# Layer-2 tile conversions placed between the links of the first pair's LoRA chain, tile by tile in a mixed pair, with the first split and the layer-3 loads moved ahead

## The reference

```python
def _L0_cond_ref(x, weight, bias, lora_a_weights, lora_b_weights, scaling_factors, adapter_id):
    base = jnp.einsum('bsi,oi->bso', x, weight) + bias
    low = jnp.einsum('bsi,bri->bsr', x, lora_a_weights[adapter_id])
    delta = jnp.einsum('bsr,bor->bso', low, lora_b_weights[adapter_id])
    return base + scaling_factors[adapter_id][:, None, None] * delta
...
x = x + _L0_cond_ref(x, ..., itok_B_1_7)     # 8 adapters of rank 16
x = x + _L1_cond_ref(x, itok_B_6_15, ...)    # the same form, 32 adapters of rank 16, own weight and bias
x = x + einsum('bsi,boi->bso', x, weight2[itok_B_3_7])   # one of 8 matrices of 1024 x 1024
x = x + einsum('bct,bcd->bdt', x, weights3[itok_B_0_15]) # 64 x 64 on the row axis
```

## Time and profile before

| | us |
|---|---|
| median of 3 runs | 655.12 |
| lowest, highest | 651.77, 655.34 |
| profiled execution, its own time | 655.87 |
| its span in the trace | 653.7 |
| PE busy, share of the span | 612.1, 94% |
| DVE busy | 297.5, 46% |
| ACT busy | 214.4, 33% |
| POOL busy | 50.3, 8% |

### The profile page before, as it was taken

The page is one execution under the profiler, slowest core; times in us unless marked ns, Lnnn a source line. Parts: engine busy times, 40 slices in busy tenths (PEclk is TensorE's granted clock), DMA queues, the critical chain, the costliest instruction groups (busy, mean ns, idle before and its releaser), DMA issues.

```text
span 653.7 us, 10849 instructions
## 1 busy us (share of the span) xinstructions
PE 612.1 (94%) x2834; PEld 505.4 (77%) x2835; DVE 297.5 (46%) x554; ACT 214.4 (33%) x306; POOL 50.3 (8%) x87
## 2 busy tenths in 40 slices
PE   5999999999938999999999998999998989999994
PEld 4888878888827888878888887888887756888882
DVE  4992211040464558254356724544863473534210
ACT  3642211040351346222335422323642352333021
POOL 4220001000010011000002100000200030000000
PEclk7999999999987999999999998999999798999997
DMA  7655723021057325733323473233348342221102
GB/s 267 228 181 59 87 82 131 31 84 65 1 181 160 120 63 192 203 100 107 97 85 109 162 227 100 77 102 101 125 134 214 107 160 81 66 87 29 34 2 66
DMA packets 70620, 73.61 MB, mean 113 GB/s; under 512 B 43586, under 2 KB 51778, under 8 KB 70596
## 3 DMA queue, kind: packets, MB, share of 16 engines
q1 hardware_dynamic: 70596, 73.32, 38.8%
HBM read 62.03 MB, written 11.27 MB: 112 GB/s over the span
## 4 chain that ended last, share of the span: by engine, by line
issue 46%; PE 37%; DMA 6%; DVE 3%; POOLq 3%; SPq 2%; POOL 1%; ACT 1%; DVEq 0%; ACTq 0%
PE y_ps L975 10%; PE y_ps L1023 6%; PE t_ps L975 5%; PE y_ps L1052 4%; PE y_ps L957 3%; DMA arena<-wt 3%; POOLq L215 2%; DMA arena<-d_tab 2%; PE t_ps L957 2%; DVE ring L820 2%; PE low_ps L957 2%; PE t_ps L1074 1%; PE low_ps L1014 1%; PE t_ps L966 1%; POOL arena L428 1%
## 5 line engine op out<-in xcount | busy, mean ns | idle before, releaser
L1052 PE MATMUL y_ps<-ring,ops 128*128 128x512 f32 (+1 forms) x792 | 188.3, 394 | 4.0 <-DVE ring L820 3.9
L1023 PE MATMUL y_ps<-wm,ops 128*128 128x512 f32 x768 | 183.7, 396 | 0.0
L1052 PEld LDWEIGHTS y_ps<-ring,ops 128*128 128x128 f32 (+1 forms) x792 | 145.5, 186 | 38.5 <-DVE ring L820 4.8
L1023 PEld LDWEIGHTS y_ps<-wm,ops 128*128 128x128 f32 x768 | 146.1, 192 | 30.5
L975 PE MATMUL y_ps<-ring,wm 128*128 128x512 f32 x240 | 55.3, 390 | 0.0
L820 DVE TENSOR_TENSOR ring<-arena,ring 128x1024 fp32r<-128x1024 f32 x40 | 48.1, 1250 | 14.0 <-ACT ring L526 12.5
L778 DVE SCALAR_TENSOR_TENSOR ops<-arena,b_is_lo,ops 128x1040 fp32r<-128x1040 f32 x16 | 20.8, 1299 | 73.9 <-ACT ops L520 73.9
L975 PEld LDWEIGHTS y_ps<-ring,wm 128*128 128x128 f32 x240 | 44.9, 188 | 9.3
L526 ACT CAST ring<-arena 128x1024 fp32r<-128x1024 f32 x40 | 40.5, 1049 | 24.8 <-POOL arena L428 23.7
L766 DVE TENSOR_TENSOR ops<-arena,ops 128x512 fp32r<-128x512 f32 x32 | 21.9, 691 | 55.3 <-ACT ops L504 55.3
L520 ACT ACTIVATE ops<-arena,b_sign 128x1040 fp32r<-128x1040 f32 x16 | 18.7, 1166 | 82.6 <-DMA arena<-d_tab 81.3
(11 more groups left out here) (143 smaller groups left out, 572.5 us busy)
## 6 DMA issues: line engine op xcount, KB each, us to landing
arena<-wt SPq DMA_DIRECT2D x48, 512.0 KB, 5.4
arena<-b_tab SPq DMA_DIRECT2D x32, 256.2 KB
arena<-xt SPq DMA_DIRECT2D x32, 256.0 KB, 2.9
arena<-b_tab SPq DMA_DIRECT2D x32, 256.0 KB
out<-arena SPq DMA_DIRECT2D x30, 256.0 KB, 3.7
arena<-w SPq DMA_DIRECT2D x8, 576.0 KB, 4.1
a_stage<-a_tab SPq DMA_DIRECT2D x64, 64.0 KB, 1.9
arena<-a_cols SPq DMA_DIRECT2D x8, 256.0 KB, 2.7
```

Source lines behind the costliest of these rows:

```text
L1023: op = nc.tensor.matmul(y_ps[:, cols], xs[:, k, part_x, :], wm[:, k, part_w, cols], start=k == 0 and part_x == part_w, stop=False)
L1052: op = nc.tensor.matmul(y[0:m, cols], xs2[:, k, part_x, 0:m], ring[:, k, part_w, cols], start=k == 0 and part_x == part_w, stop=k == KT - ...
```

## The change

1. Pair 0: instead of `convert(0, range(KT))` after everything of step 0, ACT and DVE convert two tiles at a time at four places: (0, 1), (2, 3) and (4, 5) in step 0 (DVE does (4, 5) in step 1, behind `low(1, 0)`), and (6, 7) in step 1 behind `a_hi(2)` and `a_lo(2)`.
2. Mixed pair: `quarters` is replaced by `tile_used` (one increment a tile), `half_used` and `l2_done`; ACT's `convert_mixed` waits for each tile alone. `half_used` is given by the first matmul of the second half, which stands behind the transposes.
3. Launch: A columns have semaphores `a1_in` of their own and their cast stands ahead of the fold; PE's high-by-high products wait only for `w0_hi`; `w0_lo` comes before the `b0_side` part; `start_the_order` follows the slots; 11 warm-ups in place of 9.
4. SP: `load_w3(j-1)` stands before `store(j-2)`.

```diff
-WARM_UPS = 9
+WARM_UPS = 11
...
-                sp.dma_start(slot(k)[:, FEATS + N0_COLS:], a1_cols[k]).then_inc(slot_in[k % STAGES], 16)
+                sp.dma_start(slot(k)[:, FEATS + N0_COLS:], a1_cols[k]).then_inc(a1_in[k % STAGES], 16)
...
-                    store(j - 2)
                     sp.wait_ge(w3_lo_ready, j - 1)
                     load_w3(j - 1)
+                    store(j - 2)
...
-            store(PAIRS - 2)
             sp.wait_ge(w3_lo_ready, PAIRS - 1)
             load_w3(PAIRS - 1)
+            store(PAIRS - 2)
...
             for k in range(KT):
+                act.wait_ge(a1_in[k % STAGES], 16 * (k // STAGES + 1))
+                nc.scalar.copy(a1[:, k, 0, :], slot(k)[:, FEATS + N0_COLS:]).then_inc(a1_hi, 1)
                 act.wait_ge(w0_folded, k + 1)
-                nc.scalar.copy(a1[:, k, 0, :], slot(k)[:, FEATS + N0_COLS:])
-                nc.scalar.copy(w0_blocks(k, 0), slot(k)[:, 0:FEATS].rearrange("p (i m) -> p i m", m=P))
-                nc.scalar.copy(b0_side[:, 0, k, :], slot(k)[:, FEATS:FEATS + N0_COLS]).then_inc(w0_hi, 1)
+                nc.scalar.copy(w0_blocks(k, 0), slot(k)[:, 0:FEATS].rearrange("p (i m) -> p i m", m=P)).then_inc(w0_hi, 1)
+                nc.scalar.copy(b0_side[:, 0, k, :], slot(k)[:, FEATS:FEATS + N0_COLS]).then_inc(b0_hi, 1)
...
+            def convert_mixed(rank, j):
+
+                for k in range(KT):
+                    act.wait_ge(tile_used, KT * j + (k + 1))
+                    convert(rank + 1, (k,))
+
             def xs2_hi(j, h):
                 act.wait_ge(t_done, j + 1)
                 if not (isinstance(j, int) and j == 0):
-                    act.wait_ge(quarters, 4 * j + (h - 1))
+                    act.wait_ge((half_used, l2_done)[h], j)
...
                     second_half_of_next(j - 2)
+                if before == 0:
+                    act.wait_ge(product_done, DONE_M + KT)
+                    convert(0, (0, 1))
                 if not last:
                     a_hi(j + 1)
...
                 if before == 1:
+                    convert(0, (6, 7))
                     xs2_hi(0, 0)
                     xs2_hi(0, 1)
                 if not last:
-                    for h in range(2):
-                        x_hi(j + 1, h)
+                    x_hi(j + 1, 0)
+                    if before == 0:
+                        convert(0, (2, 3))
+                    x_hi(j + 1, 1)
                     b_hi_parts(j + 1)
                 if before == 0:
-                    act.wait_ge(product_done, DONE_M + KT)
-                    convert(0, range(KT))
+                    convert(0, (4, 5))
                     return
...
                 with act.If(mixed != 0):
-                    act.wait_ge(quarters, 4 * j - 3)
-                    convert(rank + 1, FIRST_HALF)
-                    act.wait_ge(quarters, 4 * j - 2)
-                    convert(rank + 1, SECOND_HALF)
+                    convert_mixed(rank, j - 1)
...
                 low(j, 0)
+                if before == 0:
+                    convert(0, (0, 1))
+                if before == 1:
+                    convert(0, (4, 5))
...
             masks()
-            start_the_order()
             for k in range(KT):
                 split_slot(k)
+            start_the_order()
...
             def a1_products():
                 for k in range(KT):
+                    pe.wait_ge(w0_hi, k + 1)
+                    for i in range(KT):
+                        nc.tensor.matmul(PASS1[i], wm[:, i, 0, k * P:(k + 1) * P], a1[:, k, 0, :], start=k == 0, stop=False)
                     pe.wait_ge(w0_lo, k + 1)
                     for i in range(KT):
-                        for part_w, part_a in SPLIT:
+                        for part_w, part_a in SPLIT[1:]:
...
+                            if final and k == HK and part_x == part_w and cols is BANKS[0]:
+                                op.then_inc(half_used, 1)
...
+                    if final and k == KT - 1:
+                        op.then_inc(l2_done, 1)
+                    elif tiles:
+                        op.then_inc(tile_used, 1)
```

More of the change, by code:

```diff
@@ L183, in build @@
         ones_ready = sem("ones_ready")
+        a1_in = [sem(f"a1_in{n}") for n in range(STAGES)]
         w0_folded, w0_hi, w0_lo = sem("w0_folded"), sem("w0_hi"), sem("w0_lo")
+        a1_hi, b0_hi, b0_lo = sem("a1_hi"), sem("b0_hi"), sem("b0_lo")
         w1_folded, w1_hi, w1_lo = sem("w1_folded"), sem("w1_hi"), sem("w1_lo")
@@ L209, in build @@
         t_done, xs2_hi_ready, xs2_lo_ready = sem("t_done"), sem("xs2_hi_ready"), sem("xs2_lo_ready")
-        quarters = sem("quarters")
+        tile_used, half_used, l2_done = sem("tile_used"), sem("half_used"), sem("l2_done")
         x3_hi_ready, x3_lo_ready = sem("x3_hi_ready"), sem("x3_lo_ready")
@@ L861, in step @@
                 if not last:
-                    for h in range(2):
-                        x_lo(j + 1, h)
+                    x_lo(j + 1, 0)
+                    if before == 0:
+                        convert(0, (2, 3))
+                    x_lo(j + 1, 1)
                 take_x2(j)
@@ L1046, in transposes, with layer2_half @@
                 op.then_inc(t_done, 1)
-            def layer2_half(y, h, m=P, marks=()):
+            def layer2_half(y, h, m=P, tiles=False, final=False):
                 for k in (FIRST_HALF, SECOND_HALF)[h]:
@@ L1053, in layer2_half @@
                                                   start=k == 0 and part_x == part_w, stop=k == KT - 1 and part_x == 1)
-                    if k in marks:
-                        op.then_inc(quarters, 1)
+                            if final and k == HK and part_x == part_w and cols is BANKS[0]:
+                                op.then_inc(half_used, 1)
+                            if tiles and final and k == KT - 1 and part_x == 1 and cols is BANKS[0]:
+                                op.then_inc(tile_used, 1)
+                    if final and k == KT - 1:
+                        op.then_inc(l2_done, 1)
+                    elif tiles:
+                        op.then_inc(tile_used, 1)
             def layer2_by_banks(y, m=P):
@@ L1088, in first_part @@
                     pe.wait_ge(w_lo, rank * KT + HK)
-                    layer2_half(y, 0, marks=marks)
+                    layer2_half(y, 0, tiles=True)
                     between()
@@ L1092, in first_part, with last_part @@
                     pe.wait_ge(w_lo, rank * KT + KT)
-                def last_part(m=P):
+                def last_part(m=P, tiles=False):
                     if last:
@@ L1097, in last_part @@
                     else:
-                        layer2_half(y, 1, m, marks=(KT - 1,))
+                        layer2_half(y, 1, m, tiles=tiles, final=True)
                 with pe.If(mixed != 0):
-                    first_part((HK - 1,))
-                    layer2_half(y, 1, marks=(KT - 1,))
+                    first_part()
+                    layer2_half(y, 1, tiles=True)
                     pe.wait_ge(w_lo, rank * KT + (KT + HK))
-                    layer2_half(y, 0, ROWS, marks=(HK - 1,))
+                    layer2_half(y, 0, ROWS)
                     pe.wait_ge(w_lo, rank * KT + (KT + KT))
@@ L1107, in layer2 @@
                 with pe.Else():
-                    first_part((HK - 3, HK - 2, HK - 1))
-                    last_part()
+                    first_part()
+                    last_part(tiles=True)
             def step(j, before=1):
```

31 lines of the change are left out of this document (16 added, 15 removed).

## The result

| | before | changed |
|---|---|---|
| median of 4 runs, us | 655.23 | 636.33 |
| lowest, highest | 651.77, 659.79 | 633.63, 637.75 |
| profiled execution | 655.87 | 633.63 |
| its span | 653.7 | 631.4 |

Each kernel has a fourth run here; with it the median before is 655.23. The changed kernel takes 0.9703 of the time before (95% interval 0.9633 to 0.9772): 19 us less by the medians, 22.2 by the two profiled executions, of which the changed one is the fastest of its four. The forecast was 629, with a range up to 636; the median lies 7 us above the forecast and 0.3 above the range's end. Executions of one kernel differ by 4 us and more here, so a profile tells only the larger terms.

A forecast was written before the change was run, and what follows sets the result against it. PE, busy 94% of the span, sets the time, so only its waits and slow stretches count. Terms 7.0 + 12.5 + 5.6 + 0.5 + 0.7 = 26.3 off 655.87 give 629.6; median forecast 629.0, range 624 to 636.

The forecast's parts named there:

- Launch: Kernel start: PE's first product at 6.75 instead of 11.78 and no clock fall, 7.0 us less, bounds 4.0 to 7.3.
- The clock rival: Launch: the clock falls in the first products in spite of full work, 3 us go, 632 us; chance 0.10.
- Pair 0: First pair: link wait 12.17, slow stretch 1.96 and transposes 0.8 go, 14.9 us less, bounds 9 to 14.9; net 12.5.
- the thinnest place: Pair 0, step 1: x2's two splits done at 192.7 against PE's need at 193.2, behind tiles 6 and 7.
- the pieces hide only in part: Tiles 6 and 7 or pair 2's B tables come late by 5 us and more; 636 us, chance 0.12.
- the forecast's own signs: Expected in the profile, among others: pair 0's layer 2 some 22 us earlier, a 1 to 3 us wait at step 2's link.
- Pair 2's B tables: Link of pair 2: PE waits 1.7 us for late tables and 0.7 for layer-3 weights, 2.4 us back, bounds 0 to 4.
- Matrix changes: After pair 5: layer-3 loads ahead of the store let POOL fold earlier, 0.5 us less, bounds 0 and 2.6.
- that the changes improve as well: Matrix changes: waits of 1.74 and 0.67 and the slow stretch go at one or two of three; 625 us, chance 0.10.
- Mixed pair: Mixed pair: ACT could start its four tiles at 523.8 instead of 526.06, 0.7 us less, bounds 0 to 1.5.
- End: Kernel end: last layer-3 weights load earlier, last copy near 644.4 instead of 650.01, 5.6 us less, bounds 5.0 to 5.8.
- the store behind the load: Every step: stores 3 us later could hold up ACT's `take_out`, up to 3 us a step, 671 us; chance 0.02.

The follow-up runs named there:

- run with x2 first: The changed kernel with tiles 6 and 7 of pair 0 converted behind the two splits of x2 in step 1, on ACT and DVE; 635.45 us, ratio 0.9698.
- kernel of 628.72 us: The changed kernel with the mixed pair's first folds earlier on GpSimd, later matrices' first tiles issued behind layer-3 load and store, and x2 split before tiles 6 and 7; ratio 0.9585.
- run with tiles late: The changed kernel with the second matrix's four early tile loads held back in step 1 until pair 1's transposes are done; 639.09 us, ratio 0.9739.
- run by halves: The changed kernel with the old counting of quarters, the mixed pair converted by halves and the half mark ahead of the transposes; 635.54 us, ratio 0.9699.
- folds first and tiles last: The changed kernel with GpSimd's first mixed-pair folds ahead of its layer-3 weights wait, and next tiles issued behind layer-3 load and store; 633.19 us, ratio 0.9644.
- folds first: The changed kernel with GpSimd folding a mixed pair's first four tiles ahead of its wait for the pair's layer-3 weights; 635.19 us, ratio 0.9671.

## Why the prediction was right, and where it was not

The median misses the forecast of 629 by 7.3 us. The profiled execution had been forecast at 629.6 and took 633.63, so 4.0 of the 7.3 lie in the terms below. The other 3.3 are scatter: the profiled execution is 2.7 below the median of the changed kernel and was 0.6 above the median before.

*Launch: right.* 6.8 of 7.0. The missing 0.24 us at PE's start (6.99 for 6.75) is for the most part the fold: 0.63 us in place of 0.46, and begun 0.08 later, while DVE's subtraction of the A columns (4.87 to 5.55) ran beside it. The Trainium skill, "SBUF — State Buffer", section "SBUF: two separate sides", has a DVE operation with two SBUF inputs and a GpSimd operation that reads SBUF shut each other out for a whole instruction. The trace agrees in kind, not in size: from 5.24 to DVE's end it would be 0.31 us, and the fold took 0.17 longer; the price by that rule had been put at 0.6. The clock rival fell: 1.00 from 8 to 16, and the 24 products of slot 0 take 5.6 us (6.99 to 12.56). But the argument held against it was wrong. The forecast took the figure of 1.00 for the warm-ups as their speed, and their own times, 421 ns and at the end 274, show that PE was slow for most of them.

*Pair 0: the gain of 14.9 was one term too good.* The wait of 12.17 went, and the transposes' 0.8. The 1.96 us between second main half and layer 2 did not: 187.97 - 179.69 is 8.28, where 8.30 was before. The slow stretch in it did go (24 matmuls in 5.70 us for 7.56), but a pause of 1.67 took its place. And 2.36 us came anew. 14.9 - 1.94 - 2.36 = 10.6, and 10.7 was measured. The step that failed is "192.7 for the two splits of x2, against PE's 193.2. That is the thinnest place." In the changed kernel's time, 6.8 us earlier, these were 185.90 and 186.30, both as forecast. But PE's queue waits for the splits first, and only behind that wait reads two table entries and branches; 187.97 - 185.90 = 2.07 us. A wait that is met 0.4 us ahead of need is 1.7 us late. The run with x2 first had the splits 2.2 us earlier and no pause: this is shown. For the second pause there is no wait in the program; it comes in a stretch where the DMA engines were 0.9 to 1.0 busy and the trace has reads of instruction blocks among them. It went when the tile loads were held back, but also in the run with x2 first, where they were not. All seven profiles with early tile loads and the late splits have it, of 1.8 to 2.6 us. That it is PE's instructions arriving late is argued, not shown; what the two pauses have to do with each other stays open.

The rival "the pieces hide only in part" stood at 636, which is the time measured, and that is luck: tiles 6 and 7 were not late, x2 was split when forecast, and pair 2's tables came early. Two of the forecast's own signs failed instead: layer 2 of pair 0 began 20.1 us earlier, not 22, and the link of step 2 did not wait.

*Pair 2's B tables: the right wait, but covered.* The loads were issued at 178.00, to the tenth what was forecast (184.8 - 6.8), and usable at 197.36, 1.7 us better. PE came to the link at 209.81, 4.2 later than forecast, since it had paused. With the pauses taken away, the waits were 2.24 + 0.69, within the bounds of 0 to 4, but with the slow stretch behind them the step cost 6.2 us more than an undisturbed one (33.2 for 27.0). In the kernel of 628.72 us it cost 2.6. How large the wait is hangs on the tables: over the twelve profiles with early tile loads they are usable 18.6 to 23.2 us after their first issue, and by the changed kernel's own 19.4 PE, without pauses, would have come to the link as it was ready, near 205.9. Two errors of opposite sign lay here, 4.3 us lost to pauses and 2.4 not paid at the link; that the net came within 1.8 us of 12.5 was luck.

*Matrix changes: mis-sized.* "I take 0.5" was a sum over one change; the two together gave -3.0, in a term that runs from -3.8 (the run with tiles late) to +0.7 us (the layer-3 load alone) over the profiles with early tile loads, so that its size here is partly chance. In nine profiles with early tile loads, the kernel before among them, the step with the change after pair 1 took 28.8 to 33.5 us, in five with late ones 27.0 to 27.6. The earlier layer-3 load does not help, since the B tables decide, and these wait behind 2 MB of tiles. The wait after pair 5 was 2.51 us, where near 1.5 had been forecast. I had named this queue but taken its length from one row. What the forecast called a rival, that the changes improve as well, needed the tiles behind the tables and not an earlier layer-3 load.

*Mixed pair: a small gain, as forecast, for the wrong reason.* It is 1.9 us in this profile for 0.7, and 0.0 in that of the run by halves. The forecast had ACT's wait for GpSimd as what gives way. It fell from 2.24 to 0.84 us; the limit is the landing of the B tables just before it, and tile by tile adds nothing.

*End: right*, 5.9 for 5.6 by the span; the last copy ends at 627.96 in place of 650.01, 22.05 us earlier, of which 16.4 had been gained before pair 15. *`half_used`* and *the store behind the load* cost nothing: in the list of ACT's waits of the changed kernel a store stands once, at the end:

```profile
ACT arena L558 <- DMA out<-arena: 0.2, 1, 0.2
```

By its parts, then, the sum of 26.3 came to 22.3 in the span: 1.8 less in pair 0, 3.5 less at the matrix changes, 1.2 more in the mixed step, 0.1 more at both ends.

## What to carry to other kernels

A wait is not met when its data is there: what the queue does between the wait and the instruction (here two table reads and branches, 2.07 us) has to fit in too; keep that much slack, or put register reads ahead of waits (not tried here). When a stall is removed, look for the next one in whatever the stalled engine now reaches earlier; here two of three repairs uncovered B tables that had landed just in time, and the third, a wait in an in-order queue, put off the tables itself. Before a wait is made finer, see that its engine comes to it before the condition is met: the finer wait in the mixed pair stood behind another one.

## What the runs showed of the hardware

- The B tables, eight DMAs of rows of at most 4 KB over 6 us of issues, took 14.8 us from first issue to use with no tile load behind them (folds first and tiles last, mixed pair), and 19.4 with four tiles of 512 KB behind (changed kernel, pair 2).
- PE's 24 matmuls took 5.60 us undisturbed, and 7.2 to 8.4 in several stretches after waits: 7.25 with a granted clock of 0.76 in the run with x2 first, after 2.24 and 0.69 us. Not every such wait is followed by this: after 2.25 and 0.67 us at the link behind pair 9 in the changed kernel the 24 took 5.80, at 0.97.
- Four folds on GpSimd took 1.85 us beside short operations of DVE (at most 0.68 us, folds first) and 3.92 beside its splits of B tables and tiles, of 1.2 to 1.5 us each with two SBUF inputs (changed kernel). That the difference is due to them is not shown apart.
- The warm-up matmuls at launch took 421 ns each for most of the stretch and 274 at its end in the changed kernel, while the clock's figure was 1.00 for all of it.
